# Self-attention's row maxima taken per head group between its steps, v's rounding on GpSimd, and the last expert's final output quarter with h stationary

## The reference, cut to what matters

```python
# self-attention: L = 8, B = 128 tokens, 16 heads of 32; fake_quant = round to 8 bits by one scale per tensor
X = fake_quant(layernorm(x) @ Wi.T + in_b)
Q, K, V = split(X)                       # all three share the scale of X
q = fake_quant(Q / sqrt(32))
attn = softmax(einsum('bqd,bkd->bqk', q, k))   # each of the 128*16 (token, head) pairs attends over L = 8
heads = fake_quant(attn @ v)
x = x + fake_quant(heads @ Wo.T + out_b)
# experts: capacity 321 rows each, the 8 experts' w1 [512, 2048], w2 [2048, 512]
h = silu(buf @ w1);  out_buf = h @ w2
x = x + sum over the two chosen experts of share * out_buf[expert, slot]
```

## Time and profile before

| what | value |
|---|---|
| runs, us | 1733.03, 1738.48, 1738.03; median 1738.03 |
| profiled execution | 1731.91 us, span 1730.2 us |
| TensorE busy (share of span) | 1621.8 us (94%) |
| VectorE | 1166.7 us (67%) |
| ScalarE | 774.5 us (45%) |
| GpSimd | 466.9 us (27%) |
| mean granted TensorE clock | 0.971 |

### The profile page before, as it was taken

How to read it: one execution, slowest core, us unless ns; L and a number is a source line. 1 busy time by engine, 2 the same in 40 slices (tenths; PEclk the granted TensorE clock), 3 DMA queues, 4 the chain that set the end, 5 groups by cost and what they waited for, 6 DMA issues and landing times. The chain is left out here.

```text
span 1730.2 us, 39796 instructions
## 1 busy us (share of the span) xinstructions
PE 1621.8 (94%) x17262; PEld 1109.3 (64%) x17262; DVE 1166.7 (67%) x1388; ACT 774.5 (45%) x979; POOL 466.9 (27%) x404
## 2 busy tenths in 40 slices
PE   6999999999999999999999999886569999999996
PEld 4666666666666666666766666664347777777774
DVE  5678568568567657657656766566787667666766
ACT  5355336335344444445435435447535344444441
POOL 2323312232232123123212247531024411101133
PEclk9999999999999999999999999996879999999998
DMA  6534343243234234233232235450048655645534
GB/s 245 126 108 111 68 108 86 62 123 86 47 98 111 47 87 114 56 87 92 59 105 74 57 87 141 104 209 3 2 140 279 203 180 182 201 171 181 192 127 110
DMA packets 102151, 202.04 MB, mean 117 GB/s; under 512 B 25739, under 2 KB 25739, under 8 KB 101850
## 3 DMA queue, kind: packets, MB, share of 16 engines
q1 hardware_dynamic: 91258, 169.49, 33.5%
q0 software_dynamic: 10720, 30.02, 6.1%
HBM read 127.36 MB, written 18.90 MB: 85 GB/s over the span
## 5 line engine op out<-in xcount | busy, mean ns | idle before, releaser
L656 DVE TENSOR_REDUCE mx<-sc 128x4 f32<-128x2048 f32 x128 | 293.1, 2290 | 65.4 <-PE sc L900 64.8
L861 PE MATMUL proj<-w_hi,ctx 128*128 128x256 f16 x2048 | 273.5, 278 | 12.6 <-ACT ctx L441 12.5
L489 ACT ACTIVATE stage_w<-sc 128x1024 f32<-128x1024 f32 x256 | 248.2, 1025 | 69.2 <-PE sc L935 68.5
L875 PE MATMUL proj<-ctx,w_hi 128*128 128x512 f16 x1024 | 253.6, 380 | 0.0
L861 PEld LDWEIGHTS proj<-w_hi,ctx 128*128 128x128 f16 x2048 | 193.2, 99 | 64.5 <-issue 40.1
L452 ACT ACTIVATE stage_w<-proj 128x512 f32<-128x512 f32 x128 | 76.4, 597 | 339.3 <-PE proj L861 339.3
L383 POOL TENSOR_TENSOR acc_g<-stage_w 128x1024 f32<-128x1024 f32 x31 | 74.0, 2389 | 472.2 <-ACT stage_w L489 472.1
L678 DVE TENSOR_TENSOR acc_v<-acc_v,stage_w 128x1024 f32<-128x1024 f32 x93 | 129.6, 1394 | 87.2 <-ACT stage_w L489 84.4
L1166 DVE SCALAR_TENSOR_TENSOR w_lo<-stage_w,w_hi 128x2048 f16<-128x2048 f32 x64 | 144.8, 2293 | 35.2 <-ACT w_hi L1160 35.1
L616 DVE SCALAR_TENSOR_TENSOR k_lo<-proj,k_hi 128x512 f16<-128x512 f32 x128 | 87.9, 687 | 117.9 <-ACT k_hi L461 117.0
L875 PEld LDWEIGHTS proj<-ctx,w_hi 128*128 128x128 f16 x1024 | 90.0, 98 | 116.5 <-issue 25.1
(11 more groups left out here) (344 smaller groups left out, 2492.5 us busy)
## 6 DMA issues: line engine op xcount, KB each, us to landing
stage_w<-in_w SPq DMA_DIRECT2D x64, 1024.0 KB, 5.6
ctx_stage<-in_ctxT SPq DMA_DIRECT2D x64, 512.0 KB, 4.4
stage_w<-k_hi SPq DMA_DIRECT2D x256, 128.0 KB, 2.4
stage_w<-k_lo SPq DMA_DIRECT2D x128, 128.0 KB, 2.4
wq_f<-in_wiT POOLq DMA_DIRECT2D x24, 256.0 KB, 4.2
xg<-xbuf POOLq DMA_DIRECT2D x28, 176.0 KB, 4.3
obuf<-o_sb POOLq DMA_DIRECT2D x28, 176.0 KB, 3.5
xbuf<-final SPq DMA_DIRECT2D x17, 256.0 KB
```

Of the source, the lines that this page charges most:

```text
L489: act.activation(probs[:, u % 4, :], unit_scores(u), ACT.Exp, scale=1.0 / sqrt(HD)).then_inc(e_ready, 1)
L656: dve.tensor_reduce(mx[:, :, kb], sc[:, :, :], AX.X, ALU.max).then_inc(m_read, 1)
L861: last = pe.matmul(out, x_part[:, kb, e, col:col + P], w_part[:, 2, e, wv], start=term == 0 and e == 0, stop=term == 2 and e == EC - 1)
L875: last = pe.matmul(proj[at % 2][:, :], w_part[:, 1, e, P * (g % G):P * (g % G) + P], x_part[:, kb, e, :], start=term == 0 and e == 0, stop ...
```

## The change

Self-attention:

- The maxima are no longer all taken before the steps. PE now does `scores_for_max(0)`, turns `mx`, does `scores_for_max(1)`, `scores_transposed(0)` and `scores_for_max(2)`, and enters the steps. Group 3 is done head by head inside steps 1 to 4 (`last_scores_for_max(j)`: one mask product and 16 small products into bank 1 of `pb`, read by a 512-column reduction, `largest_of_last`). `mx` is turned and split three times, not once; it is set to zero at the start by a new memset. `m_hi` and `m_lo` have two places each.
- DVE rounds q of group 0 and k of groups 1 to 3, ACT rounds k of group 0 and q of groups 1 and 2, DVE rounds q of group 3 last, just before its part of the steps.
- POOL rounds all eight tiles of v, from the moment q of group 0 is done; ACT rounds none.
- `times_v` uses bank 0 of `pb` only, so it waits for the copy of the step before.

Last expert:

- PE does output 2 before hidden 3. `last_output` first adds the transpose of the four column tiles to the three row tiles in PSUM (12 f32 products with the identity), then adds output quarter 3 with h as the stationary and w2 as the moving operand: per row tile 4 x 3 products of 512 columns. Each row tile's end is signalled by itself. 48 products of 321 columns and 12 transposes become 12 f32 and 36 f16 products.
- ACT and DVE split weight quarter 7 before silu and `split_h` of quarter 3. DVE adds tiles 0 to 3 before that, and sets the adds of tiles 4 to 7 between and behind the four chunks of h. The factor 1/`WSCALE` moves from `read_column` into the scaling of `final`.

```diff
-                gp.wait_ge(k_ready, G - 1)
-                for n, g in enumerate(range(4, B)):
+                gp.wait_ge(k_ready, 1)
+                for g in range(B):
...
+                k_0 = qk[:, EC, :]
+                act.activation(k_0, k_0, ACT.Identity, bias=up, scale=inv["x"][:, :]).then_inc(q_step, 1)
+                act.wait_ge(q_step, 1)
+                act.activation(k_int[:, 0, :], k_0, ACT.Identity, bias=down).then_inc(q_ready, 1)
+                for n, f in enumerate((1, 2)):
...
-                for n in range(2):
-                    v_n = v_val[:, 2 * n:2 * n + 2, :]
...
+                quantise_q(0)
                 quantise_k(1)
+                largest_scores(0)
+                split_largest(0)
+                largest_scores(1)
                 quantise_k(2)
...
+                largest_scores(2)
+                quantise_k(G - 1)
+                split_largest(1)
+                quantise_q(G - 1)
...
                 for s in range(NS):
+                    if s == 4:
+                        largest_of_last(3)
                     invert(s)
+                    if 1 <= s < 4:
+                        largest_of_last(s - 1)
+                    if s == 4:
+                        split_largest(2)
                     if s:
                         normalise(s - 1)
...
+                def last_scores_for_max(j):
+                    pe.wait_ge(m_read, 3 + j)
+                    if j == 0:
+                        pe.wait_ge(m_split, 2)
+                        pe.wait_ge(k_ready, G + 1)
+                    own_positions(pb[:, 1, :], j)
+                    for i in range(8):
+                        for h in range(2):
+                            last = half_scores(pb[:, 1, :], G - 1, i, h, j)
+                    last.then_inc(m_ready, 1)
...
-                for f in range(G):
-                    scores_for_max(f)
-                pe.wait_ge(m_read, G)
-                pe.transpose(pt[0][:, 0:P], mx[:, :, :].rearrange("p j i -> p (j i)"), ident[:, :]).then_inc(m_turned, 1)
-
+                scores_for_max(0)
+                turn_largest(pa[:, 0, 0:P], 1)
+                scores_for_max(1)
                 scores_transposed(0)
+                scores_for_max(2)
                 for s in range(NS):
                     if s + 1 < NS:
                         scores_transposed(s + 1)
+                    if s == 0:
+                        turn_largest(pb[:, 1, 0:P], 3)
+                    if s == 4:
+                        last_scores_for_max(3)
                     times_v(s)
                     denominators(s)
+                    if 1 <= s < 4:
+                        last_scores_for_max(s - 1)
+                    if s == 4:
+                        turn_largest(pb[:, 1, 0:P], G + 3)
                     if s:
                         widen(s - 1)
...
                 def last_output(e):
...
+                    for i in range(CT):
+                        if i == CT - 1:
+                            pe.wait_ge(a_done, 16 * e + 16)
+                        for j in range(EC):
+                            pe.wait_ge(ot_ready, EC * e + j + 1)
+                            pe.matmul(turned[i][0:ROWS[i], P * j:P * j + P], ot_sb[:, j, P * i:P * i + ROWS[i]], ident[:, :],
+                                      start=j == 0, stop=False)
                     wait_split(e, s)
...
+                    for i in range(CT):
                         for f in range(4):
+                            pe.wait_ge(h_ready, 16 * e + 4 * (FQ - 1) + f + 1)
                             at = 4 * ((FQ - 1) % 2) + f
...
+                            for n, (h_part, w_part) in enumerate(mm_terms(h_hi, h_lo, w_hi, w_lo)):
+                                last = pe.matmul(turned[i][0:ROWS[i], :], h_part[:, at, P * i:P * i + ROWS[i]],
+                                                 w_part[:, s % NSPLIT, f, :], start=False, stop=f == 3 and n == 2)
+                        last.then_inc(o_turned, 1)
```

179 lines of the change are left out of this document (91 added, 88 removed).

## The result

The change took 1723.89 us (median of 5 runs, 1720.93 to 1729.35), beside 5 runs of the kernel before with median 1735.2 (1732.83 to 1738.48): ratio 0.9936, 95% interval 0.9914 to 0.9958. Run again beside 26 runs of the kernel before (median 1733.54) it gave 0.9951 (0.9936 to 0.9967), 8.5 us. My difference of 8.3 us lies in both intervals; the absolute time did not.

A forecast was written before the change was run, and what follows sets the result against it. TensorE was taken to bound the steps and experts but not the maxima stage, and the end to be its own chain. Self-attention 6.0 plus tail 2.3 gave 8.3 less: 1738.03 - 8.3 = 1729.7 us, range 1725.5 to 1736.5.

The forecast's parts named there:

- The level: Whole kernel: the change's median would lie 6 us above its profiled execution, as before, so 1738.03 is the starting time.
- The self-attention term: Maxima and steps of self-attention: 8.8 - 1.8 - 1.0 = 6.0 us less, bounds 4.5 and 7.0.
- The head start at the scores of step 3: Self-attention steps: scores of step 3 start at 1192.6 against 1201.34, 8.8 us ahead.
- I move the rise by as much as the start of that run: Self-attention: TensorE's clock rise moves with the start of its gapless run, from 1197.60 to 1189.1.
- the prediction's time: Times in the change's trace less 8.53 us, because self-attention started that much later there, in unchanged code.
- the losses: Self-attention steps: three more single-head rounds cost 1.8 us, the third turn and split with its wait 1.0.
- The tail: Last expert to the third indirect add at the program's end: 2.3 us less, bounds 0 and 2.4.
- Rival 2: Last expert: f32 products' loads not hidden, PE ends 2.6 later, tail gives nothing; 6.0 less in total, 1732.0; chance 0.10.
- The signs: Trace events in self-attention and tail named beforehand as showing the forecast right, such as POOL's v done before 1187.
- 1 (no overlap of the small products): Single-head rounds: 16 products run one behind the other, 1.08 us more a round; 4.0 less in total, 1734.0; chance 0.12.
- 3 (VectorE falls behind): Self-attention maxima: POOL costs each k pass 0.7 and reaches into q 3; 2 to 3 less gain, 1732.2; chance 0.05.
- 4 (the clock stays down): Self-attention steps: clock does not rise, a step takes 7.3 instead of 3.9 us; up to 1753.7; chance 0.05.

The follow-up runs named there:

- after_again: The changed kernel run again as it is, against the kernel before: 1725.68 us, ratio 0.9951.
- tail_only: Kernel before with only the last expert changed, self-attention as before: 1730.56 us, ratio 0.9979 to the kernel before.
- sa_only: Changed self-attention with the last expert of the kernel before: 1728.7 us, ratio 0.9968 to the kernel before.
- after_warm: Changed kernel plus unread products (128x128 on 512 columns) in TensorE's waits behind self-attention: 1723.84 us, ratio 0.9952 to the kernel before.
- heads_twice: Changed kernel with each single-head round (mask product and 16 small products) issued twice: 1727.93 us, ratio 0.9966 to the kernel before.
- after_filled: Changed kernel plus unread whole products in TensorE's waits behind self-attention and ahead of its scores: 1721.9 us, ratio 0.9929 to the kernel before.
- before_filled: Kernel before plus unread whole products (128 rows, 512 columns) in TensorE's waits of the maxima stage: 1734.46 us, ratio 0.9999 to the kernel before.
- group3_whole: Changed kernel with the last head group's maxima taken in one piece ahead of the first sums with v: 1730.72 us, ratio 0.9984 to the kernel before.
- before_warm: Kernel before with own-position products of the first three head groups run nine times instead of once: 1734.45 us, ratio 1.0004 to the kernel before.

## Why the prediction was right and where it was wrong

**The level failed, and with it the range.** The step is "The median of the runs is 6 us above that execution, and I expect that of the change to be as well: 1738.03 - 8.3". The 1738.03 was the middle one of three runs; the medians of before with more runs were 1735.2, 1733.54, 1732.96 and 1733.47. From 1733.5 the same sum gives 1725.2, between the two measured medians of the change, 1723.89 and 1725.68. I had named the spread (5.4 among three runs) and set the low end only 3 us under the forecast's best bound. The profiled execution, 1731.91, spoke for a lower level too, and I argued it away; for the change the offset even has the other sign, its profiled execution, 1729.35, lies 5.5 above its median. Of the 5.8 us between 1729.7 and 1723.89, the level is 2.8 (1738.03 to 1735.2) and the difference 3.0 (11.3 instead of 8.3). Of these 3.0 the traces show 1.6: 1.7 more in self-attention, 0.1 less in the tail. The rest lies within the scatter of the runs.

**The self-attention term was too small.** 6.0 was forecast with bounds 4.5 to 7.0, 7.70 was seen. Step by step:

- The head start at the scores of step 3 was 8.8 in the prediction; it is 39.38 - 29.73 = 9.65 (1201.34 and 1200.22, each from its stage's start). The premise that failed is "I move the rise by as much as the start of that run", a run without a gap, to 1189.1. In the change TensorE had pauses of 0.7 to 1.2 us, was busy 7.03 of 9.54 us, and ran without a gap only from 1189.88 (its own time), 3.4 us ahead of the rise, where before it was 5.8; in the prediction's time the clock was up at 1184.8. So the denominators of step 0 were out of the way early, and what set the start of step 1's was VectorE and not TensorE's own chain: it was done with q of group 3 at 1188.1 instead of 1188.7 (GpSimd cost it 0.3 less than charged, the rest are small sizes), its first reciprocal ended at 1188.9 instead of 1189.6, and the denominators of step 1 started at 1189.0 instead of 1190.0.
- Then the losses: 2.8 forecast (1.8 for three rounds, 1.0 for the third turn and its wait). Measured 0.68 + 0.68 + 1.55 = 2.91, the last being a round, a turn of 0.26 and a wait of 0.64. This part holds, though a round is 0.68 and not 0.6.
- The remaining 0.94 are stalls of the kernel before in two of its steps, which my 3.89 from the earlier trace rows did not contain. 0.85 + 0.94 - 0.11 is the 1.7 that the term was short. How much of them an execution has is not in the code alone: the change had none in its steps, after_again, the same kernel, had 2.9.

Those stalls come and go. Over the executions with the code of either side, the stage took 66.23 and 67.04 before (tail_only), 58.53, 61.46, 58.86 and 58.50 now (after_again, sa_only, after_warm): 66.6 against 59.3 on average, 7.3. With 2.2 of the tail that is 9.5, between the 8.5 and 11 of the two comparisons.

**The tail held, row by row.** In the prediction's time (here 0.53 is added, by the end of output 1) the last add to x ends at 1714.3 (forecast 1714.5), the register move is at 1716.4 (1716.6), the first add starts at 1717.25 (1717.45), the third at 1721.4 (1721.3). The f32 products took 2.65 (2.6). One order is other than forecast: the third add waited for its row tile, scaled at 1720.6 instead of 1720.3, and not for POOL's queue. The two were forecast 0.1 us apart, so the time is the same. Rival 2 is refuted.

**The signs.** First exponential ended by 1181.3: 1181.29. v done before 1187: 1182.4. Clock 1.00 by 1190: 1184.8. Steps with a round at 4.5, later ones at 3.9: 4.57 twice, 5.44 with the third turn and its wait, then 3.89. Head maxima 6 earlier: 7.7. Third add 2.3 earlier: 2.2. Of the rivals, 1 (no overlap of the small products) is refuted by heads_twice, 3 (VectorE falls behind) is refuted by the 0.9 us that GpSimd cost, 4 (the clock stays down) by the rise.

**What stays open.** TensorE's stalls inside the steps. In the steps with a round they were absent in the change, sa_only and after_warm (4.57 each) and small in others (0.2 in one step of after_again, 0.6 in one of after_filled); where steps of 3.89 follow one another most executions have them. The DMA view of before_filled over 30 us of its steps shows one more thing that goes on there:

```profile
q8 instruction: 8, 0.13, 1.8%
```

Eight packets of 16 KB in 30 us, about one a step. The change has the same packets without a stall, seven in the 25 us from 1200. A step of 3.89 us holds 148 products in the records (38 per us), one with a round 165 in 4.57 (36 per us). That TensorE's instructions at times arrive too slowly for the first rate would explain why a step cannot stay at 3.89, and why group3_whole and before_filled got nothing back. No run changed how the instructions arrive, so this is a reading and not shown. Nor do I know whether runs without the profiler have these stalls; the equal medians of before and before_filled would fit that, but a cost of the fillers themselves would look the same.

## What to carry to other kernels

Forecast the difference from the trace, but take the level from all runs that are to be had: three runs with a spread of 5 us can be off by more than a small change is worth. Work done by one engine in one block ahead of a pipeline is best split and laid in the pipeline's steps, even where each piece costs the bound engine its full price (four rounds of 0.68 against 6.6 us at the start). And a shorter way to the first step is only worth what the steps behind it can take up: before_filled started 1.2 to 2.2 us earlier and ended no earlier.

## What was not expected of the hardware

- TensorE loses 0 to 3 us in eight steps of small products without a wait that the profile knows, in the same code and differently in each execution (steps of 28.09 and 30.99 us in the change).
- With whole products of 512 columns in TensorE's waits the clock's last rise came at 26.2, with rounds of four products of 9 rows at 33.0, though with these TensorE was busy 4.99 of 5.00 us between 1180 and 1185 of before_warm; and even whole ones left dips to 0.50 within the stage.
- Sixteen products of 64 columns on one row group take 0.37 us, 23 ns each, at full clock.
- GpSimd's pass and VectorE's pass over SBUF slow each other (GpSimd 1.06 instead of 0.69, VectorE 1.07 instead of 0.69), but a reduction of VectorE from PSUM leaves GpSimd at 0.69. What a pass loses is 0.1 to 0.2 less than the rest of the other engine's pass that it meets.
